# Edge loop of a graph layer: three PSUM banks for the partial sums, each addition one item step later, two users of one bank

## What is computed

```python
feat_src = (feat @ W_n).reshape(N, H, D)
e = (left[src] + right[dst] + em_e) / 3.0        # three 4-term scores an edge and head
e = jnp.where(e > 0, e, 0.2 * e)
e_max = segment_max(e, dst)
e_exp = jnp.exp(e - e_max[dst])
a = e_exp / segment_sum(e_exp, dst)[dst]
rst = segment_sum(feat_src[src] * a[:, :, None], dst)
```

## Time and profile before

| | us |
|---|---|
| median of 3 runs (4086.71 to 4087.13) | 4086.85 |
| time of the profiled execution | 4127.28 |
| span of the profiled execution | 4125.6 |
| TensorE busy in it | 3054.4 |
| VectorE busy | 1979.3 |
| GpSimd busy | 1857.8 |
| ScalarE busy | 1623.2 |

### The profile page before, as it was taken

How to read it: one execution, slowest core, us unless ns; L and a number is a source line. 1 busy time by engine, 2 the same in 40 slices (tenths; PEclk the granted TensorE clock), 3 DMA queues, 4 the chain that set the end, 5 groups by cost and what they waited for, 6 DMA issues and landing times. The chain is left out here.

```text
span 4125.6 us, 59259 instructions
## 1 busy us (share of the span) xinstructions
PE 3054.4 (74%) x12566; PEld 2356.6 (57%) x12567; DVE 1979.3 (48%) x5348; ACT 1623.2 (39%) x3631; POOL 1857.8 (45%) x1906
## 2 busy tenths in 40 slices
PE   3541777776777777777677776777765999999997
PEld 1221666565556665665566655555553677777775
DVE  6730555555555555555555555555673122222221
ACT  2311544454455444545544544455432222222221
POOL 0005456666666665666665666666254111111111
PEclk9865677777777777777767778777855999999998
DMA  7834444444444444444444444446564312121123
GB/s 221 258 138 112 123 140 130 131 128 129 131 129 130 131 130 128 132 138 130 130 131 129 130 130 130 130 129 119 75 216 136 91 31 32 31 32 31 31 32 83
DMA packets 309415, 481.35 MB, mean 117 GB/s; under 512 B 161911, under 2 KB 237507, under 8 KB 300366
## 3 DMA queue, kind: packets, MB, share of 16 engines
q0 software_dynamic: 100848, 285.40, 28.1%
q1 hardware_dynamic: 194910, 181.82, 14.5%
q10 hardware_dynamic: 13392, 11.23, 0.9%
HBM read 408.52 MB, written 76.12 MB: 117 GB/s over the span
## 5 line engine op out<-in xcount | busy, mean ns | idle before, releaser
L819 POOL DMA_INDIRECT rows<-table,idx x1664 | 1575.6, 947 | 1063.3 <-issue 445.9
L862 PE MATMUL ps_acc<-rows,hot 128*128 128x264 f32 x3328 | 1260.7, 516 | 538.5 <-DVE acc L1163 496.5
L862 PEld LDWEIGHTS ps_acc<-rows,hot 128*128 128x128 f32 x3328 | 761.9, 253 | 673.1 <-issue 566.6
L1163 DVE TENSOR_TENSOR acc<-acc,ps_acc 128x264 f32 x832 | 355.3, 427 | 987.3 <-remote 659.3
L847 PEld LDWEIGHTS ps_term<-er,hot_t 128*128 128x128 f32 x3328 | 638.1, 247 | 218.5 <-issue 146.5
L847 PE MATMUL ps_term<-er,hot_t 128*128 x3328 | 579.5, 305 | 85.7 <-issue 67.9
L1149 DVE TENSOR_TENSOR rows<-rows,ps_p 128x512 f32<-128x512 f32 x832 | 565.5, 680 | 3.8 <-ACT ps_p L971 0.5
L960 ACT ACTIVATE hot<-iota_row,neg_rel 128x128 f32<-128x128 f32 x1664 | 546.3, 388 | 8.7 <-PE ps_acc L862 8.0
L1730 PE MATMUL ps_h<-w,acc 128*128 x1680 | 528.5, 457 | 0.5 <-ACT acc L1649 0.5
L1642 POOL DMA_INDIRECT x_dram<-acc,to x105 | 161.7, 1540 | 761.8 <-ACT acc L1658 761.8
L935 ACT COPY e_t<-ps_e 128x128 f32<-128x128 f32 x208 | 56.4, 271 | 1021.6 <-remote 978.1
(11 more groups left out here) (263 smaller groups left out, 2811.9 us busy)
## 6 DMA issues: line engine op xcount, KB each, us to landing
dst_row<-rel_d SPq DMA_DIRECT2D x52, 1024.0 KB
rows<-table,idx POOLq DMA_INDIRECT x1664
rec<-rec_d SPq DMA_DIRECT2D x832, 24.0 KB
rec_d<-acc SPq DMA_DIRECT2D x16, 1050.0 KB
acc<-slots_x SPq DMA_DIRECT2D x105, 130.0 KB, 2.1
acc<-in_edge_attr_dram SPq DMA_DIRECT2D x16, 700.0 KB
wrow<-in_L_ffn_w_dram ACTq DMA_DIRECT2D x16, 640.0 KB
table<-fo SPq DMA_DIRECT2D x49, 148.0 KB
```

Of the source, the lines that this page charges most:

```text
L819: pool.indirect_dma_start(rows[:, in_ring(k) + j, :], None, table, bass.IndirectOffsetOnAxis(ap=idx[w][:, t:t + 1], axis=0)).then_inc(gath ...
L862: last = pe.matmul(ps_acc[m % 2][:, 0:PW], hot[m // QI % 2][:, m % QI * G + j, :], rows[:, in_ring(i * (2 * NI) + at) + j, 0:PW], start=(j ...
L1163: dve.tensor_tensor(so_far, so_far, ps_acc[m % 2][:, 0:PW].rearrange("p (h d) -> p h d", h=HEADS), ALU.add).then_inc(added, 1)
```

## The change

`ps_x` is given up. Its two halves become one, `x_at`, in the upper half of `ps_l`, and `back_at` is the same place: TensorE's turn back writes over the maxima that it no longer needs. The free bank becomes a third `ps_acc`. `sums` of item k goes to bank k % 3 and waits for the addition of item k - 3 instead of k - 2. `ADD_LAG` goes from 25 to 26: VectorE takes out the sum of item s - 26 in item step s. In `tops` the small product `less` (which reads `drop_at` in `ps_l`) moves ahead of the two scans and of the signal `tops_ok`.

```diff
@@ -68,7 +68,8 @@
 ROUNDS = BATCHES // 2
 LAG = 22
 SUM_LAG = 24
-ADD_LAG = 25
+ADD_LAG = 26
+SUM_BANKS = 3
 ROW_ITEMS = 36
 
 assert ROUNDS * 2 == BATCHES and EP * COLS == EDGES and PAD >= ITEM + 1 and NI * HEADS == P
@@ -681,12 +682,11 @@
             ps_e16 = ps(st, "ps_e16", [P, 512])
             ps_p = ps(st, "ps_p", [P, 512])
             ps_term = [ps(st, f"ps_term{u}", [P, 512]) for u in range(2)]
-            ps_acc = [ps(st, f"ps_acc{u}", [P, 512]) for u in range(2)]
-            ps_x = ps(st, "ps_x", [P, 512])
+            ps_acc = [ps(st, f"ps_acc{u}", [P, 512]) for u in range(SUM_BANKS)]
             ps_l = ps(st, "ps_l", [P, 512])
 
-            x_at = ps_x[:, 0:ITEM]
-            back_at = ps_x[:, ITEM:2 * ITEM]
+            x_at = ps_l[:, ITEM:2 * ITEM]
+            back_at = x_at
             p_at = ps_p[:, 0:BT * HEADS].rearrange("p (e h) -> p e h", h=HEADS)
             ends_at = ps_l[:, 0:3 * NI].rearrange("p (c i) -> p c i", i=NI)
             carry_at = ps_l[:, 64:64 + 2 * NI].rearrange("p (c i) -> p c i", i=NI)
@@ -857,9 +857,9 @@
                         pe.wait_ge(msg_ok, k1)
                         pe.wait_ge(hot_ok, i * (2 * QUADS) + (at // QI + 1))
 
-                        after(pe, added, k1 - 2)
+                        after(pe, added, k1 - SUM_BANKS)
                         for j in range(G):
-                            last = pe.matmul(ps_acc[m % 2][:, 0:PW], hot[m // QI % 2][:, m % QI * G + j, :], rows[:, in_ring(i * (2 * NI) + at) + j, 0:PW],
+                            last = pe.matmul(ps_acc[(k1 - 1) % SUM_BANKS][:, 0:PW], hot[m // QI % 2][:, m % QI * G + j, :], rows[:, in_ring(i * (2 * NI) + at) + j, 0:PW],
                                              start=(j == 0), stop=(j == G - 1))
                         last.then_inc(acc_done, 1)
 
@@ -1125,14 +1125,14 @@
                     def tops(i, w):
 
                         dve.wait_ge(carry_ps, batches(i, w, 1, 1))
+                        dve.wait_ge(first_ok, batches(i, w, 1, 1))
+                        after(dve, scale_ok, batches(i, w, 1))
+                        dve.tensor_scalar(less[:, :], drop_at, first[:, :], None, ALU.mult).then_inc(less_ok, 1)
                         step(dve.tensor_tensor(picked[:, :, :], carry_at, item_sel[:, :].unsqueeze(1).to_broadcast([P, 2, NI]), ALU.mult))
                         step(dve.tensor_reduce(carry[:, :], picked[:, :, :], AX.X, ALU.add))
                         step(dve.tensor_tensor_scan(x_at, pen_t[:, 0:ITEM], x_at, carry[:, 0:1], ALU.add, ALU.max))
                         dve.tensor_tensor_scan(top_t[:, ::-1], pen_t[:, 1:ITEM + 1][:, ::-1], x_at[:, ::-1], carry[:, 1:2],
                                                ALU.add, ALU.max).then_inc(tops_ok, 1)
-                        dve.wait_ge(first_ok, batches(i, w, 1, 1))
-                        after(dve, scale_ok, batches(i, w, 1))
-                        dve.tensor_scalar(less[:, :], drop_at, first[:, :], None, ALU.mult).then_inc(less_ok, 1)
 
                     def below_top(i, w):
 
@@ -1160,7 +1160,7 @@
                             dve.tensor_tensor(so_far, so_far, scale[:, :].unsqueeze(2).to_broadcast([P, HEADS, HDIM + 1]), ALU.mult).then_inc(rescaled, 1)
                             dve.wait_ge(rescaled, n1)
                         dve.wait_ge(acc_done, k1)
-                        dve.tensor_tensor(so_far, so_far, ps_acc[m % 2][:, 0:PW].rearrange("p (h d) -> p h d", h=HEADS), ALU.add).then_inc(added, 1)
+                        dve.tensor_tensor(so_far, so_far, ps_acc[(k1 - 1) % SUM_BANKS][:, 0:PW].rearrange("p (h d) -> p h d", h=HEADS), ALU.add).then_inc(added, 1)
 
                     def slot(i, w):
                         for v in range(QUADS):
```

## The result

The changed kernel takes 4061.08 us, median of 5 runs (4056.57 to 4070.22), against 4086.85 us before, median of 5 (4084.76 to 4102.45). The ratio is 0.9932, 95% interval 0.991 to 0.9955: faster by 26 us. That is in the stated range, but a quarter of the 99 us that the forecast took off. The profiled execution is one of 4061.08 us, span 4059.4 us; that of before was 40 us above its median, so the two traces differ by 66 us.

What follows compares the result with a forecast made beforehand. The prediction took cycles of gathers, pause and late TensorE signals to bound the edge loop. From the profiled 4127.3 us it took 99 for fewer pauses, then 40 for profiled against median time: 3988 us, range 3940 to 4095.

Steps and rivals of the forecast that it cites:

- the cycle as what bounds the loop: Edge loop: release of TensorE's held signals, eight gathers, a pause; 12.42 us for four items, 3.11 us each.
- five items in a cycle: Edge loop: a third held sum lets ten gathers pass per pause, 14.95 us or 2.99 an item; chance 0.45.
- nothing for `less`, for the shared bank and for SyncE: Moved product, shared ps_l place and SyncE's record loads were priced at zero; `less` on the path would cost 10 us.
- four and five take turns: Rival: edge-loop cycles alternate between four and five items, half the gain, 4037 us; chance 0.12.
- ScalarE pins the cycle: Rival: ScalarE's 4.5 us after a release keep one quad a cycle, no change, 4087 us; chance 0.23 with other no-effect ways.
- the length of a pause hardly depends on what the cycle held: Reason for choosing 99 us: GpSimd's pause stays 2.48 us with five items in a cycle as with four.
- The term of 99 us: Third bank and later addition: a fifth fewer GpSimd pauses, 88 us over 707 items, 99 us over 796.
- second stop: Rival: GpSimd stops again in each five-item cycle, 43 us more, 4130 us; worse above 0.6 us; chance 0.15.
- The sign of three held sums: Expected in the trace if right: VectorE makes three additions within 3 us after a release.
- the time for a fifth item: TensorE has room: idle 2.96 us a cycle plus 2.5 us more length, against 1.5 to 2.6 us an item.
- the release comes when the gathers have run dry: Edge loop: held TensorE signals arrive only after GpSimd, its ring full, stops gathering; each pause 2.48 us.
- The rule against it: Trainium skill's report that PSUM double-buffering gave no further gain; read as time staying at 4087 us.

Runs made afterwards that it cites:

- e9: The changed kernel with three banks but the addition step put back (ADD_LAG 25), on a chip with cycles: ratio 0.9952 to the kernel before.
- e10: The changed kernel with two banks of sums, the later addition step (ADD_LAG 26) kept, on a chip with cycles: ratio 1.0004 to the kernel before.
- e4: The kernel before with only the shared place in ps_l and `less` ahead of the scans, two banks, ADD_LAG 25: 4120.21 us, ratio 0.9997.
- e3: The changed kernel with ScalarE's copy of the turned edge attributes moved behind its compare and mark: 4095.38 us, ratio 0.9936 to the kernel before.
- e2: The changed kernel run again without edit, beside the kernel before on the same chip: 4097.46 us, ratio 0.9944.
- e17: The changed kernel with one 128 x 384 memset on GpSimd behind each item's two gathers: 4041.37 us, ratio 0.9891 to the kernel before.
- e18: The changed kernel with one 128 x 192 memset on GpSimd behind each item's two gathers: 4056.14 us, ratio 0.9924 to the kernel before.
- e15: The changed kernel with two 128 x 384 memsets behind each item's two gathers, on a chip with cycles: 4397.69 us, ratio 1.0778 to before.
- e12: The changed kernel with two 128 x 384 memsets behind each item's two gathers, on the chip without cycles: 4366.87 us, ratio 1.2221 to before.
- e7: The changed kernel with a fourth bank for sums, `p` in SBUF and ADD_LAG 27, on the chip without cycles: 3654.75 us, ratio 1.0227 to before.

## Why the prediction was right and wrong

**Right.** The direction; the cycle as what bounds the loop; the third bank as the part that carries the gain (e9, e10); five items in a cycle, ten gathers, 14.98 to 15.1 us on chips A and E against the 14.95 foreseen (partly luck: this was added up from cycles of eight of 12.42 us, which last 12.27 there, and on chips B and D ten take 15.3 to 15.4); nothing for `less`, for the shared bank and for SyncE (e4). On the first chip it came out as "four and five take turns", priced at 4037 us where 4061 was measured, with the sign of "ScalarE pins the cycle" in its eight-gather cycles.

**Wrong, the first step: "the length of a pause hardly depends on what the cycle held".** It does. Behind the last gather the transfers always end after 1.57 to 1.60 us (medians, before and after), but in the kernels with three banks on chips A, B, D and E the next gather comes 2.54 to 2.68 us after it behind eight and 2.84 to 3.02 behind ten. A fifth item makes a cycle 15.08 - 12.27 = 2.81 us longer, not 2.49. The term of 99 us was mis-sized by this. On chip B, which has both kernels, a cycle of ten costs 3.052 us an item at best (e3) against 3.105 before (12.42 / 4), so a loop of such cycles alone would gain 0.053 x 796 = 42 us, where the sum had 99. This was the larger error. The rival "second stop" had the threshold right (0.6 us more and ten is worse than eight); 0.3 of it came true, as a longer pause and not as a second stop.

**Wrong, the second: the cycle settles at five.** Only 66 of some 160 cycles hold ten gathers (42 on chip B). The sign of three held sums, three additions within 3 us after a release, is all but missing too: it stands at one of the 66 stops behind ten gathers (additions from 1.5 us ahead of GpSimd's next gather on), so how the fifth item comes through is not shown. With a third of the items in cycles of ten (e2), most of the 42 us is not reached; measured were 24.5 us there between the medians, with fewer short stops as another part; how the 24.5 split is not shown. That the cycle has "the time for a fifth item" counted TensorE's work, but not that it must arrive before the signals are held. ScalarE's three steps pin some cycles (the rows at 1994.06 to 1999.14). e3 showed that this pin can be taken away, that others take its place (L862 and L960 waiting again), and that little is lost by it, because ten is worth so little more than eight.

**Wrong, the reading behind both: the release comes when the gathers have run dry.** In the kernel before the two often come together, but already there 132 of the 366 late moves of `acc_done` come while packets of a gather are under way, and in e17 390 of 439 do. Nor is the cycle gathers plus a fixed pause: e18 added to the gathers, and the pause gave it back. One picture would be a path that deals with an item's signals in some 2.85 us on chips A, E and F, an estimate from the lengths: gathers at 2.50 us run ahead of it, TensorE's signals queue behind theirs, and the pause is the time to catch up. No row names such a path, and two things speak against it as the whole cause: e17, at 2.80 us an item, should have next to no held signals and has as many as the change, and an item still takes 3.03 us there. What holds the signals stays open. Shown is that spacing the items' gathers by 1.26 us ends the holding (e15).

**The profiled execution.** The sum took off the 40 us by which the profiled execution of before lay above the median. The traces differ by 66 us and the medians by 26: part of what I priced in that trace was not in the typical run. On chip B, profiled 4126.18 and 4091.68 us, the medians are 4122.0 and 4097.46. One reading, not shown, is that the profiled execution of before fell on a chip like B or D and the timed ones on one like E or F. Its cycles of eight last 12.43 us, as on B (12.42) and D (12.4 to 12.5), where the medians of before are 4122 and 4130 us. Those of the changed kernel last 12.27, as on E and F, where they are 4085 and 4084; on B the change alone moves them by only 0.04. The difference of 0.16 us is worth an estimated 0.04 x 796 = 32 us of the 40. So the sum subtracted the 40 us rightly for the median, but the rows it was built from may belong to a slower chip.

**The range and the signs.** The range's ends were added up loosely: half way from 3988 to 3923 is 3956 us, not 3940, and no change with 10 us for `less` is 4097, not 4095. Neither bears on the outcome. GpSimd's idle time fell to 832 us, not 807, and an item takes 3.04 us, not 2.99.

**The rule against it.** The third bank gave 0.5 to 0.7% on chips A, B, D and E and nothing on C (0.9995). The Trainium skill (TensorE: Matmul & The Clock Gate, section HAM oscillation) reports PSUM double-buffering as no further gain, and its own two times, 126.6 and 125.5 us, lie 0.9% apart. A gain of the size found here would not count there, so these runs do not contradict it; the prediction took it for a stronger rule than it is.

**Left open.** Why the chips differ; what holds the signals; how much of the gain each kind of cycle carries; four banks and a smaller ring on a chip with cycles. e17 is the fastest version against its own before, 0.9891 against 0.9936 and 0.9932 for the change, but on another chip, and its interval touches the change's (0.992 and 0.9919), so that it beats the change was not measured side by side. On chip F it is 15 us below e18 (4041.37 and 4056.14). On a chip like C its 2.80 us an item would stand against 2.50, an estimated 0.30 x 832 = 250 us slower.

## What to carry to other kernels

When signals arrive in a bunch, don't price the cycle as work plus a fixed pause: compare cycles that held different amounts, since the trace of before had some of six, eight and ten gathers (9.49, 12.43 and 15.89 us), and the 2.94 to 3.46 us between them, not 2.49, was what an item more costs. A wait that ends last on an engine (448 us for L1163) is worth what the thing behind it lets go: 366 us of it went and 26 us were won. And before tuning to a rhythm, see whether another chip has it: the third bank gave 0.5 to 0.7% on the chips with cycles and nothing on chip C.

## What the hardware showed that I had not expected

- One program, one launch, the same inputs: 3573 us on one chip and 4084 to 4130 us on the others. With the gathers spaced by 1.26 us (e12, e15) no signal is held on either kind of chip and the difference shrinks to 31 us, though GpSimd then sets the pace of the loop and could hide others.
- Signals can be late where the work is not: matmuls that ended at 1964.64 us moved their semaphore at 1968.89.
- Slowing GpSimd down by 0.30 us an item (e17) did not slow the kernel: it ran 1.1% faster than the kernel before, against 0.6 to 0.7% for the change alone on other chips. The signals are still held, but GpSimd stops for long 55 times instead of some 160.
- A memset of 0.17 us behind a gather moves the next one by 0.02 us; one of 0.27 by 0.14, one of 0.43 by 0.30. The 0.30 us that GpSimd leaves before the next gather can hold other work.
- `p` in SBUF instead of PSUM (e7, with a fourth bank, chip C) made the gathers 49 ns longer on average, those beside VectorE's product 102 ns, and the kernel 2.3% slower.
